# Last projections of a transformer pair on one Trainium2 core: the rounding of the hidden units moves from VectorE to ScalarE

## The reference, cut to what matters

```python
h = einsum('bsd,dh->bsh', layernorm(x), W_exp) + b_exp   # 256 -> 1024
h = butterfly(h, up_weights, 1024)
h = gelu(h + up_bias, approximate=False)
h = butterfly(h, down_weights, 1024)
x = x + tanh(g_ffn[1]) * (einsum('bsh,hd->bsd', h, W_con) + b_con + down_bias)
```

## Time and profile before

| what | value |
|---|---|
| median of 3 runs | 1375.49 us (1370.84 to 1376.63) |
| the profiled execution, its own time | 1384.0 us |
| its span, first to last instruction | 1382.4 us |
| mean granted TensorE clock | 0.902 of full |
| PE / DVE / ACT / POOL busy, whole span | 82% / 59% / 53% / 27% |
| loads of ScalarE's function tables | 33, of 1.28 us: 15 before a gelu (L1215), 15 before an exponential behind it (L1185), 3 elsewhere, one of them ahead of the 32 silus of the shared expert (L1097) |
| chain that ended last, by engine | PE 56%, DVE 22%, ACT 8%, issue 6%, DMA queues and DMA 8% |

### The profile page before, as it was taken

One profiled execution on the slowest core, in us unless ns is written; L12 is line 12 of the kernel. 1 busy time (PEld: TensorE's weight loads), 2 busy tenths in 40 slices (PEclk: granted clock), 3 DMA queues, 4 the chain that ended last, 5 costly groups with the idle time before them and its releaser, 6 DMA issues.

```text
span 1382.4 us, 18017 instructions
## 1 busy us (share of the span) xinstructions
PE 1127.2 (82%) x5921; PEld 806.6 (58%) x5921; DVE 814.3 (59%) x2040; ACT 732.4 (53%) x1439; POOL 378.2 (27%) x320
## 2 busy tenths in 40 slices
PE   5697778877886398998899958879898978888887
PEld 3363544444443276887678747647575756666566
DVE  4386487587675676546554457565565556555443
ACT  2686578678784354656565521443444444443542
POOL 3101001101100001677677520123232231312233
PEclk9697898899997599999999979779997999999998
DMA  8324324324200502687887461130403041210000
GB/s 252 88 65 122 90 90 122 87 93 122 62 35 19 211 21 88 163 204 191 224 202 189 81 162 46 55 96 1 117 1 111 3 115 35 78 48 16 18 16 16
DMA packets 89898, 129.74 MB, mean 94 GB/s; under 512 B 20496, under 2 KB 59792, under 8 KB 89552
## 3 DMA queue, kind: packets, MB, share of 16 engines
q1 hardware_dynamic: 77520, 109.73, 26.7%
q0 software_dynamic: 12288, 18.88, 7.6%
HBM read 72.18 MB, written 30.70 MB: 74 GB/s over the span
## 4 chain that ended last, share of the span: by engine, by line
PE 56%; DVE 22%; ACT 8%; issue 6%; SPq 4%; DMA 4%; POOL 1%; DVEq 0%; ACTq 0%; POOLq 0%
PE psum L975 6%; PE psum L960 5%; PE psum L805 4%; PE psum L715 4%; PE psum L710 4%; SPq L1806 4%; PE psum L821 4%; PE psum L879 4%; PE psum L692 3%; PE psum L908 3%; PE psum L840 3%; PE psum L888 2%; DVE weights L1344 2%; PE psum L681 2%; DVE stats L1243 2%
## 5 line engine op out<-in xcount | busy, mean ns | idle before, releaser
L692 PE MATMUL psum<-q_stack,k_stack 96*128 96x512 f32 (+1 forms) x256 | 136.8, 549 | 55.1 <-DVE weights L1344 28.3
L1691 POOL TENSOR_SCALAR vareps<-moments 128x4 f32<-128x4 f32 x32 | 8.2, 255 | 623.1 <-DVE moments L1246 623.1
L1593 DVE TENSOR_REDUCE peaks<-psum 128x2 f32<-128x308 f32 x256 | 108.8, 469 | 41.8 <-PE psum L910 41.7
L908 PE MATMUL psum<-k_stack,q_stack 96*128 96x256 f32 x256 | 90.2, 400 | 52.0 <-DVE peaks L1593 21.2
L692 PEld LDWEIGHTS psum<-q_stack,k_stack 96*128 96x128 f32 (+1 forms) x256 | 53.5, 213 | 111.3 <-DVE weights L1344 46.5
L1724 POOL DMA_INDIRECT expert_sums<-made,sum_rows x64 | 104.9, 1639 | 48.9 <-DVE made L1563 28.3
L715 PE MATMUL psum<-weights,values 128*32 128x512 f32 x512 | 108.2, 703 | 9.1 <-DVE weights L1344 9.1
L1185 ACT ACTIVATE weights<-psum 128x512 f32<-128x512 f32 x160 | 92.1, 595 | 42.1 <-PE psum L692 36.6
L1749 POOL TENSOR_TENSOR hidden<-hidden_whole,hidden 128x512 fp32r<-128x512 f32 x64 | 82.1, 1283 | 107.0 <-DVE hidden L1641 107.0
L1344 DVE SCALAR_TENSOR_TENSOR weights<-psum,weights 128x512 f32<-128x512 f32 x160 | 107.0, 679 | 5.3 <-ACT weights L1047 4.8
L805 PE MATMUL psum<-feat_parts,w_shared_up 128*128 128x512 f32 x384 | 99.5, 410 | 9.3 <-DVE feat_parts L1451 8.2
(11 more groups left out here) (190 smaller groups left out, 2575.9 us busy)
## 6 DMA issues: line engine op xcount, KB each, us to landing
q_stack<-q_stage SPq DMA_DIRECT2D x192, 128.0 KB, 2.4
expert_w<-in_expert_w SPq DMA_DIRECT2D x64, 384.0 KB
expert_sums<-zeros SPq DMA_DIRECT2D x6, 1408.0 KB, 7.1
fetched<-expert_sums SPq DMA_DIRECT2D x16, 512.0 KB, 4.9
wk_stack<-in_wk SPq DMA_DIRECT2D x16, 384.0 KB, 3.9
rows_scratch<-rows SPq DMA_DIRECT2D x8, 640.0 KB, 3.4
k_raw<-in_k SPq DMA_DIRECT2D x16, 300.0 KB
x<-in_x SPq DMA_DIRECT2D x8, 512.0 KB, 6.5
```

The source lines that it names most:

```text
L692: T.matmul(to, k[0:row, head, :], q[0:row, head // 2, :], start=True, stop=True).then_inc(scored, 1)
L908: T.matmul(view[:, :, 0:P], q[0:STACK, p, t * P:(t + 1) * P], keys[0:STACK, 2 * p:2 * p + 2, :], start=True, stop=True)
L1593: V.tensor_reduce(peaks[h % 2][:, t, 2 * p:2 * p + 2], view, AX.X, ALU.max).then_inc(wide.frees(key, i), 1)
```

## The change

The rounding of each block leaves VectorE's program and goes into ScalarE's, right behind the block's gelu. It takes both waits with it: the one for the out unit that last read the buffer, and the one for the gelu itself (the bank's free semaphore), which ScalarE now raises and waits for itself. VectorE's list of units has no "up" any more. GpSimd, TensorE, the buffers, the semaphores and the order of the units stay.

```diff
@@ scalar_program
             def up(h, k):
-                n, key = HB * h + k, ("up", h, k)
+                n, b, key = HB * h + k, (2 * h + k // BURST) - 1, ("up", h, k)
                 if n >= 2:
                     A.wait_ge(hid_split, n - 1)
                 A.wait_ge(*wide.filled(key))
                 A.activation(whole[n % 2][:, :], wide.ap(key), ACT.Gelu,
                              bias=hid_bias[:, k:k + 1]).then_inc(wide.frees(key), 1)
+                if b >= 0:
+                    A.wait_ge(out_made, BURST * b + k % BURST + 1)
+                A.wait_ge(*wide.freed(key))
+                A.activation(hidden[k % BURST][:, 0, :], whole[n % 2][:, :], ACT.Copy).then_inc(hid_cast, 1)
@@ vector_program
-            def up(h, k):
-                n, b = HB * h + k, (2 * h + k // BURST) - 1
-                if b >= 0:
-                    V.wait_ge(out_made, BURST * b + k % BURST + 1)
-                V.wait_ge(*wide.freed(("up", h, k)))
-                V.tensor_copy(hidden[k % BURST][:, 0, :], whole[n % 2][:, :]).then_inc(hid_cast, 1)
-
@@
-                     "turn_f": turn_f, "up": up, "out": out_add}
+                     "turn_f": turn_f, "out": out_add}
```

## The result

The changed kernel took 1383.28 us in the median of 17 runs (1375.61 to 1386.59), the kernel before 1375.49 in 17 runs beside them. The ratio is 1.0043 with a 95% interval of 1.0028 to 1.0057: 5.9 us slower, between 3.9 and 7.8. The two medians lie 7.8 us apart, at the upper edge of that. 4.2 was forecast.

The account below looks back on a forecast made before the run. A loop through three banks (gelu 1, up 2, gelu 2, up 3) was taken to bound bursts with peaks. Terms 3.2 + 0.6 + 0.4 = 4.2 us slower, 1379.7 from the median; range 1371 to 1386.

Parts of the forecast that it names:

- The copy: ScalarE's new rounding behind each gelu: 0.62 us, 0.52 to a gelu behind it; 0.72 at the upper end.
- The wait for its own gelu: On ScalarE, the copy waits for the gelu ahead of it: 0.03 us, and the overlap of the two lost.
- First kind: Six bursts with a late table load, gelus 0 and 1 back to back: net 0.53 us slower each, 3.2 together.
- Peak 1's wait: In six bursts, peak 1 was held up by VectorE's 1.50 us cast; without it 0.13 us gained each.
- Second kind: Five bursts where gelu 1 already waits for its product: 0.12 us slower each, 0.6 together.
- Bursts without peaks: Four bursts; in the two with attention beside them the exponential comes 0.43 us later, costing 0.2 each, 0.4 together.
- The last round's "nothing": Nothing waits for an exponential there and TensorE's four outs cover GpSimd's rest 3: no cost and no gain.
- VectorE's relief: VectorE loses 46.0 us of casts, worth only the 0.13 counted at peak 1; it would wait longer for products.
- the rival "faster": VectorE reaches its maxima sooner, TensorE waits less: 1366.6 us if all 8.9 us of waits went; chance 0.08.
- Exponentials in bursts with peaks: Copy 3 delays them by 0.65 us, but this is covered; without cover twelve bursts would pay up to 7.8.
- The clock: Rival: the lower clock stays through six bursts after a longer pause at up 2, 18 us, about 1398; chance 0.06.
- The tables: Rival: the copy needs another table, so loads stand in each of 64 blocks, some 160 us; chance 0.01.

## Why the prediction was right

The measured 5.9 us lie near the forecast 4.2, in its range, and the sign and the mechanism were those of the text. By the medians it is 7.8, a little above the upper end of 7.4. By its steps:

- **The copy**, 0.62 us, took 0.63. **The wait for its own gelu**, 0.03, took 0.09, because there are two waits and not one. The pair of the first stage from which I took it had one. A nearer row stood in the earlier trace rows: VectorE's cast, with the same two waits, starts at 1132.81, 0.10 us behind gelu 0's end at 1132.71.
- **First kind**, 0.53 us each, measured 0.62 in the burst shown and 3.4 in the six for 3.2. Up 2 came later by 0.73 and not 0.66, mostly through that gap. Peak 1's wait went as said.
- **Second kind**, 0.12, measured 0.14 in the burst shown and 0.7 in the five for 0.6. The stage's first burst showed no cost.
- **Bursts without peaks**, 0.2 each, measured 0.61: the mis-sized term. The path through copy 0, the rests, gelu 3 and copy 3 was the right one, but it grew by 0.61 us up to the exponential (9.01 behind the first up before, 9.62 after) and not by 0.43, and I had forgotten TensorE's own price of a wait: on the chain the product L692 takes 0.50 us when it had to wait and 0.23 in line, where it starts under the product ahead of it, so the little slack ahead of it bought nothing. The last round's "nothing" can't be judged from these profiles: its 0.56 us are the clock's, from before the round's first copy.
- **VectorE's relief** was worth the 0.13 at peak 1, and nothing else that the traces tie to the change: the rival "faster" had its place right and no more. Its busy time fell by 39.8 us and not by 46; why was not followed.
- **Exponentials in bursts with peaks** were covered: no score product waits for one within 12 us of out 0, before or after. Only the two bursts without peaks have new waits, of 0.11 us.
- **The clock** did not cost time in the changed kernel's profiled bursts with peaks. It did in three of six with 0.53 us more of pause, and in two of six with the same pause and other copies. The forecast stood nearer to that edge than its 0.06 said.
- **The tables**: 33 loads before and after.

## What to carry to other kernels

Before work is moved to an engine that is idle for half of the time, look at what stands next in that engine's order and whether someone waits for it: here one extra copy of 0.6 us behind the first gelu of a burst cost some 12 us in all, and twice as many behind the second and third nothing that the runs show. Where such a spot hurts, look for what made it late; here the table load, taken ahead of the waits, gave back 10.2 us in the changed kernel, more than the 5.9 of the engine's choice, and 4.7 in the kernel before. And follow every loop that passes the moved step, since putting the copy one place later freed one loop and closed another.

## What the runs showed of the hardware that wasn't expected

- A wait on ScalarE that has long been met still costs 0.06 us when it is the second in front of an instruction (0.09 against 0.03 us from gelu to copy).
- A product of TensorE that had to wait adds more to the chain: 0.50 us against 0.23 for the same L692. In line it lasts 0.40 us in the timeline (1320.23) and overlaps the product ahead of it; behind a wait it lasts 0.50 (1319.55) and overlaps none. The ends of products are modelled in these profiles.
- The lower clock can fall inside a burst, with up units of 2.31 us in place of 1.65: in three of six bursts with a wait of 1.40 us at up 2, in none of the changed kernel's six with 0.89 us, and in two of six of another run with the same 0.89 us.
